# ScalarE in place of VectorE for the PSUM evacuation of q, k and v in the small attention without rotary positions

## What is computed

```
x = x + attn_a(layernorm(x))          # wide attention, rotary
x = x + l0_ffn(layernorm(x))          # 16-head attention (8 wide), then 8 experts, top 1
x = x + attn_b(layernorm(x))          # wide attention, alibi
x = x + l0_ffn(layernorm(x))
x = x + l1_attn_a(layernorm(x))       # 16 heads of 8, rotary, causal
x = x + l1_ffn(layernorm(x))          # 16 heads of 8 with biases, then 8 experts, top 2
x = x + l1_attn_b(layernorm(x))       # state space, grouped rotary attention, dense
x = x + l1_ffn(layernorm(x))
```

## Time and profile before

| | |
|---|---|
| median of 3 executions | 4941.18 us |
| span of the profiled execution | 4944.1 us |
| TensorE busy | 3835.4 us (78%) |
| VectorE busy | 3465.1 us (70%) |
| ScalarE busy | 2341.8 us (47%) |
| GpSimd busy | 2386.9 us (48%) |
| L522 in both l0att stages | 512 times, 687 ns each |
| L522 in both l1ffn stages | 512 times, 686 ns each |
| bounce<-parts, one DMA | 256 KB, 2.8 us from issue to landing |

### The profile page before, as it was taken

How to read it: one execution, slowest core, us unless ns; L and a number is a source line. 1 busy time by engine, 2 the same in 40 slices (tenths; PEclk the granted TensorE clock), 3 DMA queues, 4 the chain that set the end, 5 groups by cost and what they waited for, 6 DMA issues and landing times. The chain is left out here.

```text
span 4944.1 us, 90876 instructions
## 1 busy us (share of the span) xinstructions
PE 3835.4 (78%) x25840; PEld 2735.3 (55%) x25840; DVE 3465.1 (70%) x9524; ACT 2341.8 (47%) x5537; POOL 2386.9 (48%) x3900
## 2 busy tenths in 40 slices
PE   7889797779999799568869937567775887799365
PEld 5666565656666466456646626422332665466265
DVE  7887775666666676566658856669998664588566
ACT  3444464355666466234436624345553454366243
POOL 5666442534344442446643354367776662233453
PEclk9999898789999899679979959779998999899698
DMA  6000332100000232133323311212121330133113
GB/s 234 0 0 1 112 124 76 52 20 1 0 0 1 72 124 94 39 124 107 107 80 117 110 38 47 73 48 65 63 62 64 114 117 28 51 120 112 36 46 87
DMA packets 244547, 341.24 MB, mean 69 GB/s; under 512 B 26976, under 2 KB 187120, under 8 KB 243120
## 3 DMA queue, kind: packets, MB, share of 16 engines
q1 hardware_dynamic: 230960, 309.19, 18.8%
q0 software_dynamic: 13184, 27.22, 1.6%
HBM read 182.77 MB, written 147.26 MB: 67 GB/s over the span
## 5 line engine op out<-in xcount | busy, mean ns | idle before, releaser
L522 DVE TENSOR_REDUCE l0att_rowmax<-l0att_S 128x2 f32<-128x512 f32 x512 | 339.8, 687 | 125.2 <-PE l0att_S L701 122.9
L893 POOL TENSOR_TENSOR wb_prob<-wb_prob,wb_rden 128x128 f32<-128x128 f32 (+1 forms) x512 | 248.2, 506 | 360.7 <-DVE wb_rden L1070 360.3
L522 DVE TENSOR_REDUCE l1ffn_rowmax<-l1ffn_S 128x2 f32<-128x512 f32 x512 | 337.6, 686 | 87.2 <-PE l1ffn_S L701 83.1
L1983 POOL TENSOR_TENSOR ssm_hc<-core_AW_all,ssm_Cs 128x512 f32<-128x512 f32 x256 | 320.8, 1268 | 131.2 <-DVE core_AW_all L2129 98.1
L1434 POOL DMA_INDIRECT results<-e_y,e_back x220 | 213.7, 971 | 289.4 <-DVE e_y L1662 269.9
L935 ACT ACTIVATE wb_prob<-wb_biased,wb_nmax 128x128 f32<-128x128 f32 (+1 forms) x512 | 228.6, 447 | 236.0 <-DVE wb_nmax L1063 233.6
L2228 PE MATMUL ssm_Y<-ssm_hc,core_ident 128*128 128x512 f32 x512 | 287.8, 672 | 56.8 <-POOL ssm_hc L1983 31.1
L2129 DVE TENSOR_TENSOR_SCAN core_AW_all<-core_AW_all,ssm_U 128x512 f32<-128x512 f32 x256 | 310.6, 1213 | 1.0 <-ACT core_AW_all L2072 0.6
L701 PE MATMUL l1ffn_S<-l1ffn_K,l1ffn_Q 128*128 128x512 f32 x512 | 251.0, 494 | 75.1 <-DVE l1ffn_rowmax L522 42.3
L1775 PE MATMUL e_H<-e_xT,e_W1s 128*128 128x128 f32 x1760 | 252.0, 288 | 70.2 <-issue 50.6
L701 PE MATMUL l0att_S<-l0att_K,l0att_Q 128*128 128x512 f32 x512 | 248.6, 489 | 60.4 <-DMA l0att_K<-bounce 47.5
(11 more groups left out here) (498 smaller groups left out, 11511.3 us busy)
## 6 DMA issues: line engine op xcount, KB each, us to landing
bounce<-l0att_parts SPq DMA_DIRECT2D x128, 256.0 KB, 2.8
bounce<-l1ffn_parts SPq DMA_DIRECT2D x128, 256.0 KB, 2.8
ssm_Cs<-c_rows SPq DMA_DIRECT2D x128, 256.0 KB, 3.1
routed<-core_Y SPq DMA_DIRECT2D x8, 2048.0 KB, 24.8
l0att_Q<-bounce SPq DMA_DIRECT2D x128, 128.0 KB
l0att_K<-bounce SPq DMA_DIRECT2D x128, 128.0 KB
bounce<-l1att_parts SPq DMA_DIRECT2D x64, 256.0 KB, 2.8
l1ffn_Q<-bounce SPq DMA_DIRECT2D x128, 128.0 KB
```

The costliest lines, as they stand in the source:

```text
L522: dve.tensor_reduce(out=rowmax[:, jp, qt, 2 * pair:2 * pair + 2], in_=S[a % 2][:].rearrange("p (j k) -> p j k", j=2)[:, :, 0:keys(qt)], op ...
L893: ins = pool.tensor_tensor(out=prob[:, w_ % NP, a:b], in0=prob[:, w_ % NP, a:b], in1=rden[:, w_ % NP, n:n + 1].to_broadcast([P, b - a]), o ...
L1983: pool.tensor_tensor(out=hc[:, u % 4], in0=hs[:, u % 4], in1=Cs[:, n % 4], op=ALU.mult)\
```

## The change

In the stages without rotary positions, q and k are taken out of PSUM by ScalarE instead of VectorE; so is v, in every stage where v has no bias. By the code the second condition holds for l0att0, l0att1 and also for gqa, which is rotary. On ScalarE q is `scale * x` (a Copy with a constant scale) or `scale * x + scale * bq` (an Identity with a scaled bias column, computed once in the stage by one small instruction), k is a Copy or an Identity with bias. Slots, banks, waits (`given`, `parted`, `weighed`) and the signal `gone` stay as they are; only the engine that performs them changes. In l1ffn v keeps its place on VectorE.

```
+        bq_scaled = sb("bq_scaled", [P, 1]) if not rope and bq is not None else None
...
             # ScalarE
+            if not rope and bq is not None:
+                act.activation(bq_scaled[:], bq, ACT.Copy, scale=q_scale).then_inc(scaled.sem, 1)
...
+                    elif x == "qk":
+                        given(n, x)
+                        await_(act, parted, parted.at(n - 1))
+                        if bq is None:
+                            act.activation(full[:, 0, :], F[:, 0:L], ACT.Copy, scale=q_scale)
+                            act.activation(full[:, 1, :], F[:, L:2 * L], ACT.Copy).then_inc(gone(x, n), 1)
+                        else:
+                            if n == 0:
+                                act.wait_ge(scaled.sem, 1)
+                            act.activation(full[:, 0, :], F[:, 0:L], ACT.Identity, scale=q_scale, bias=bq_scaled[:])
+                            act.activation(full[:, 1, :], F[:, L:2 * L], ACT.Identity, bias=bk)\
+                                .then_inc(gone(x, n), 1)
+                    elif x == "v" and bv is None:
+                        given(n, x)
+                        await_(act, weighed, weighed.at(n - 3, 2))
+                        act.activation(Vp[:, n % 3, :, :, 0:DH], F[:, 0:L].rearrange("p (t h d) -> p t h d", t=QT, h=H),
+                                       ACT.Copy).then_inc(gone(x, n), 1)
...
             # VectorE
-                    if x == "qk":
-                        dve.wait_ge(f_made.sem, turn_of[x, n] + 1)
-                        await_(dve, parted, parted.at(n - 1))
-                        dve.tensor_scalar(full[:, 0, :], F[:, 0:L], bq if bq is not None else 0.0, q_scale, ALU.add,
-                                          ALU.mult)
-                        dve.tensor_scalar(full[:, 1, :], F[:, L:2 * L], bk if bk is not None else 0.0, None,
-                                          ALU.add).then_inc(gone(x, n), 1)
...
-                    elif x == "v":
+                    elif x == "v" and bv is not None:
...
-                        else:
-                            dve.tensor_copy(dst, got).then_inc(gone(x, n), 1)
```

More of the change, by code:

```diff
@@ L529, in after_slot @@
                     F = bank(x, n)
-                    if x == "qk":
-                        dve.wait_ge(f_made.sem, turn_of[x, n] + 1)
-                        await_(dve, parted, parted.at(n - 1))
-                        dve.tensor_scalar(full[:, 0, :], F[:, 0:L], bq if bq is not None else 0.0, q_scale, ALU.add,
-                                          ALU.mult)
-                        dve.tensor_scalar(full[:, 1, :], F[:, L:2 * L], bk if bk is not None else 0.0, None,
-                                          ALU.add).then_inc(gone(x, n), 1)
-                    elif x in ("qq", "kk"):
+                    if x in ("qq", "kk"):
                         k = x == "kk"
@@ L558, in after_slot @@
                         got = F[:, 0:L].rearrange("p (t h d) -> p t h d", t=QT, h=H)
[L559 to L562, removed]
-                        else:
-                            dve.tensor_copy(dst, got).then_inc(gone(x, n), 1)
+                        dve.tensor_tensor(out=dst, in0=got,
+                                          in1=bv[:].rearrange("p (h d) -> p h d", h=H)[:, None]
+                                          .to_broadcast([P, QT, H, DH]), op=ALU.add).then_inc(gone(x, n), 1)
                     elif x in ("n0", "n1"):
```

## The result

The changed kernel takes 4955.65 us (median of 15 executions, 4950.79 to 4960.98) against 4944.33 us for the kernel before in the same comparison (15 executions, 4932.66 to 4950.57). The ratio is 1.0024, with a 95% interval from 1.0016 to 1.0031: 11 us more, where 3 us less were forecast. Every one of the 15 executions is longer than each of the 15 of the kernel before. The profiled execution has a span of 4952.1 us, 8.0 us above the one of before.

A forecast was written before the change was run, and what follows sets the result against it. The prediction took TensorE to lead, with VectorE near it in l1ffn0 and ScalarE about 37% free. Steady rounds 0, v 0 and openings 3.0 us gave 4941.2 - 3.0 = 4938.2 us, range 4928 to about 4946.

The forecast's parts named there:

- Part 1, steady rounds: q and k in 64 steady rounds: ScalarE's idle time covers the moved pair, VectorE's freed time gives nothing; 0 us.
- Part 2, v: v without bias, 48 rounds in l0att0, l0att1 and gqa: ScalarE's added copy is covered by existing waits; 0 us.
- Part 3, openings: Opening of each l1ffn stage: part(0) starts 1.5 us earlier, the DMA chain follows; 3.0 us gained, nothing in l0att0.
- the hop to GpSimd: l1ffn openings: the step from ScalarE's end of q and k to GpSimd's part(0), estimated at 0.1 us.
- The mis-sized term: l1ffn openings: VectorE clears K for sequence 1 some 0.9 us sooner, so its store just fits behind SyncE's sends.
- rival (a): l1ffn openings give nothing, as sequence 1 or the DMAs behind the stores bind; 4941 us, chance 0.22.
- The sum: Whole kernel: 0 + 0 + 3.0 us gained, 4941.2 - 3.0 = 4938.2 us.
- The rival on the slower side (c): Steady rounds: a late exponential makes TensorE wait for its bank, 0.3 us in 64 rounds; 4960 us, chance 0.08.
- The range: Whole kernel: the time was expected between 4928 and about 4946 us.
- a busy share of 85%: One l1ffn0 stretch: VectorE busy 60.6 of 71.0 us, near TensorE's 64.1 us.

The follow-up runs named there:

- fill76: The changed kernel with 76 one-column memsets added to VectorE's stream in the first l0att stage: 4941.57 us, ratio 0.9992 to the kernel before.
- late: The kernel before with the change in all stages but the first l0att stage: 4941.93 us, ratio 0.9994.
- late_order: `late` with ScalarE's long rows of sequence 1 written behind its q and k instead of ahead: 4938.28 us, ratio 0.9994 to the kernel before.
- all_order: The whole change with the 76 memsets of `fill76` and the order of `late_order`: 4941.18 us, ratio 0.9994 to the kernel before.
- experiment 10: The run of `late_order`, 4938.28 us; its table compares l1ffn0 and l1ffn1 opening times in five kernels.
- experiment 9: `late` with two more 128x256 Copies on ScalarE behind each q and k pair, 48 rounds: 4938.63 us, ratio 0.9997 to the kernel before.

## Why the prediction was wrong, by its own steps

**Part 1, steady rounds: right.** The Copies take 385 and 377 ns and the Identities 475 and 467 ns; 0.385 and 0.47 us were taken.

```profile
L480 ACT ACTIVATE l0att_full<-l0att_F x32: 384/385/386, 511.2 to 1936.0; 128x256 f32<-128x256 f32 x32
L481 ACT ACTIVATE l0att_full<-l0att_F x32: 377/377/378, 511.4 to 1936.3; 128x256 f32<-128x256 f32 x32
```
```profile
L485 ACT ACTIVATE l1ffn_full<-l1ffn_F,l1ffn_bq_scaled x32: 474/475/476, 2548.3 to 4543.6; 128x256 f32<-128x256 f32 x32
L486 ACT ACTIVATE l1ffn_full<-l1ffn_F,core_cols x32: 467/467/468, 2548.7 to 4544.0; 128x256 f32<-128x256 f32 x32
```

They stand in the idle time of the earlier trace rows, of which 0.25 us are left ahead of them. The copies behind keep 0.69 and 0.62 us, the last of them that of mt0, on which SyncE's loop hangs:

```profile
712.54 0.39 ACT L480 ACTIVATE l0att_full<-l0att_F 128x256 f32<-128x256 f32 x1 [0.25 <-PE l0att_F L672]
712.82 0.38 ACT L481 ACTIVATE l0att_full<-l0att_F 128x256 f32<-128x256 f32 x1
713.08 0.60 ACT L519 ACTIVATE l0att_probT<-l0att_T 128x512 f32<-128x512 f32 x1
714.37 0.39 ACT L503 ACTIVATE l0att_onT<-l0att_F 128x256 f32<-128x256 f32 x1 [0.69 <-PE l0att_F L694]
...
716.05 0.37 ACT L497 ACTIVATE l0att_maxT<-l0att_F 16x256 fp32r<-16x256 f32 x1 [0.62 <-PE l0att_F L682]
```

On VectorE the freed time became idle time, as forecast: ahead of the maximum of slot 11 it grew from 0.59 to 1.15 us, and 0.64 us stand ahead of the maximum of slot 10, where before 0.41 us stood ahead of the pair:

```profile
2699.14 0.69 DVE L542 TENSOR_REDUCE l1ffn_rowmax<-l1ffn_S 128x2 f32<-128x512 f32 x1 [0.64 <-PE l1ffn_S L711]
2700.98 0.69 DVE L542 TENSOR_REDUCE l1ffn_rowmax<-l1ffn_S 128x2 f32<-128x512 f32 x1 [1.15 <-PE l1ffn_S L711]
```

**Part 2, v: right.** The strided copy takes 390 ns, inside 0.385 to 0.43, and the rounds of l0att are as long as before. The gqa stage takes 344.5 to 350.0 us in the six kernels with its v on ScalarE and 345.6 to 349.5 us in the seven others. The Identities reload no table: the exponentials of the changed kernel (L519) load one twice, as before.

**Part 3, openings: right in sign and size, with one term off.** Of l1ffn0 after the change, the rows that answer to the earlier trace rows:

```profile
2544.59 3.70 ACT L449 ACTIVATE l1ffn_K<-core_pick 4x2048 fp32r<-4x2048 f32 x2 [0.64 <-DVE l1ffn_K L623]
...
2549.30 0.61 POOL L376 CAST l1ffn_parts<-l1ffn_full 128x512 fp32r<-128x512 f32 x1 [1.36 <-ACT l1ffn_full L486]
...
2555.91 3.70 ACT L449 ACTIVATE l1ffn_K<-core_pick 4x2048 fp32r<-4x2048 f32 x2 [5.53 <-DVE l1ffn_K L631]
...
2561.40 0.60 SPq L299 DMA_DIRECT2D l1ffn_K<-bounce  x1
2562.58 0.37 SPq L280 DMA_DIRECT2D bounce<-l1ffn_parts  x1
...
2563.66 1.22 PE L711 MATMUL l1ffn_S<-l1ffn_K,l1ffn_Q 128*128 128x512 f32 x2 [9.86 <-DMA l1ffn_K<-bounce]
```

part(0) comes 4.71 us after the first long row, forecast 4.7; the hop to GpSimd, estimated at 0.1 us, takes 0.14 us from the end of k (2548.69 + 0.47) to 2549.30. The first scores come 19.5 us after it on average over the two l1ffn stages of the six kernels that have the change there (19.0 to 20.0), against 20.7 us in the seven that don't (20.4 to 21.3): 1.3 us sooner in each stage where 1.5 was taken. The length of the stage, from its first matmul to that of the next stage, points the same way. l1ffn1 takes 330.0 to 330.9 us in the six and 331.6 to 333.4 us in the seven; l1ffn0 takes 331.2 and 332.9 us on average, with some overlap. In the total time this gain is not clear of noise: the intervals of `fill76`, `late`, `late_order` and `all_order` all hold 1.000.

The mis-sized term is how much sooner the rows of sequence 1 come: they start 11.32 us after the first long row instead of 11.59, so 0.27 us sooner and not 0.9. The store of sequence 1 therefore comes late. SyncE has issued its last send by 2562.00 us and waits until 2562.58, and in `late_order`, where nothing holds the store up, it comes at 17.44 us (l1ffn0) and 17.09 us (l1ffn1) instead of 17.99 and 17.98. This is the sign that the prediction named for rival (a), and it did appear. But its consequence did not: the first scores came sooner all the same, and bringing the store forward brought them no further forward (the table of experiment 10). In l0att the change gave nothing, as forecast (first scores at 18.91 and 19.05 us, before 18.96 and 19.09).

**The sum: the step that failed.** "0 + 0 + 3.0 us" took the path of each changed stage and set the rest of the kernel at nothing, without giving a reason. The missing term is the position of VectorE's later code: 16.5 us in wb. With it the working gives -3.0 + 16.5 = 13.5 us, inside the measured 8 to 15 us. In the two profiled executions 16.5 - 3.5 = 13.0 us (3.5 us is what the first scores of both l1ffn stages gained in them) stand against 8.0. The other 5 us are left open as scatter: the rotary l1att stage, in which nothing is changed, took 366.9 us before and 361.4 after, and 361.4 to 373.1 us over the thirteen profiles. The rival on the slower side (c) had the right sign with the wrong mechanism, so its 0.08 is no credit: among TensorE's waits in both stretches there is none for an exponential, and experiment 9 excludes it. The range ended at 4946 us because its upper end held only the spread of three executions and l1ffn's openings (4941.2 + 2.2 + 1.8 = 4945.2).

What could have been seen ahead: the page of the kernel before lists instruction packets, and none in the turns of wb, where VectorE has a loop of 364 instructions. That its place leaves room for less than 16 instructions could not be read from that profile. That removing 76 shifts it could be, and this was a rival worth a chance, though its price of 16.5 us was not to be had from the rows.

## What to carry to other kernels

When instructions are removed or added on an engine, ask which loops stand behind them in that engine's program. Compare the instruction packets and the length of those loops' turns before and after, whatever the edit was meant to do: here 76 instructions fewer cost 16.5 us in a stage that the edit doesn't touch. Moving 0.95 us a round off VectorE gave nothing in l1ffn, where VectorE had caught up with TensorE (0.59 us idle) before the next thing that somebody waits for. That idle time, tested by adding work ahead of it (0.97 us in each of 48 rounds, at most 2.5 us in the total), told this better than a busy share of 85%.

## What the runs showed of the hardware

- A loop of 364 records on VectorE had turns of 78.4 us and no instruction packet in them with shifts of 0, +4 and +128 instructions in VectorE's program, and five packets of 8 KB in every turn, two or three of them at the jump, with -76, +16 and +52. A turn with packets and a clock of 1.00 was 2.3 us longer (80.7 us; 81.0 us with +16).
- In one turn 2.08 us without a matmul were followed, 0.7 us after work had begun again, by 3.6 us at a mean granted clock of 0.53; the turn was 1.6 us longer than one with the stall alone (82.3 against 80.7 us). In another turn of the same loop the clock stayed at 1.00 though TensorE had stood for 2.30 us. Why isn't shown. The second turn:

```profile
1258.00:1260.00 2.00, 1.34 (x6) 0.60 (x4) 0.00 (x0) 0.00 (x0) 0.00 (x0) 1.00 0.00 0
1260.00:1262.00 2.00, 0.36 (x3) 0.31 (x3) 1.68 (x7) 0.92 (x4) 0.88 (x2) 1.00 0.02 4
1262.00:1264.00 2.00, 2.00 (x14) 1.12 (x13) 1.24 (x7) 1.65 (x6) 1.07 (x3) 1.00 0.00 0
```
```profile
1261.64 0.52 PE L1186 MATMUL wb_T<-core_ident,wb_prob 128*128 128x128 f32 x3 [2.30 <-DVE wb_probT L1085]
```
